# Eight sparse tiles of a graph layer, fetched row by row by SyncE instead of by GpSimd

## The chip, the cores and the metric

One core of a Trainium2 chip runs the kernel. The metric is the device time of one execution, in microseconds (us). Five engines work side by side, each through its own program in order: TensorE (PE in the profile; its weight loads PEld), VectorE (DVE), ScalarE (ACT), GpSimd (POOL) and SyncE (SP), which only issues transfers. They wait for each other by semaphores. A transfer adds 16 to its semaphore when it has landed.

## The reference

A graph with 12500 nodes of 128 features and 200000 edges, sorted by destination, each with a type of 9. The message of an edge is its source's row through a linear layer plus an embedding of its type; messages are summed by destination, and a GRU cell with the node's own row gives the update; the result is added to x and normalized.

```python
src_h = h[src] @ W_msg.T + b_msg
emb = edge_embed[jnp.clip(edge_type, 0, NUM_EDGE_TYPES)]
msg = src_h + emb
messages = jax.ops.segment_sum(msg, dst, num_segments=num_nodes)
h_new = _gru_cell(messages, h[:num_nodes], W_ih, W_hh, b_ih, b_hh)
...
x = _layernorm(x + _L0_gnn_ref(x, edge_index, edge_type_9, ...), axis=-1)
```

## The kernel before, in words

As the layers are linear, the kernel sums the sources' rows and the counts of edge types for each destination first, and applies the weights to the sums. The destinations are treated in two ways.

*Dense part.* The first 3328 nodes have about half of the edges. For them one-hot matrices are made on VectorE (items `B`, lines 862 to 887), turned into a matrix of counts on TensorE (line 1099), copied to SBUF by ScalarE (line 1226), and multiplied with all of x (items `F`, line 1114). This needs no fetching of rows.

*Sparse part.* The other edges stand in 764 tiles (`NG`) of 128 edges, four to a group, 191 groups (`GROUPS`). For each tile the 128 source rows are fetched to a buffer of `xg`, which has 17 (`RING`): GpSimd issues one indirect DMA a tile (`gather`, line 601, recorded at line 604), after a wait on `s_used` for the buffer 17 tiles back to be free. The first 22 groups (`SWITCH`) fetch the fp32 rows of x itself. The others fetch from `x_split`, a tensor in HBM in which each row of x stands as three bf16 parts, 768 bytes in all, and which SyncE writes at the start from SBUF (lines 542 to 550, semaphore `s_xw`). TensorE multiplies the three parts of each tile with a one-hot matrix (line 1081) and adds `G` = 4 to `s_used` behind each group's last product (line 1085). VectorE adds each group's sums to a ring (line 906), at an offset from a register: it loads four such offsets at a time (line 890).

*Final stages.* The nodes are finished in 49 blocks (`NBLK`) of 256, in the order `ORDER`. A block passes the stages `cn`, `hh`, `su`, `rz`, `t2`, `th`, `yt`, `bn`, `sd`, `ln`: two sets of products on TensorE (`hh`, line 1042, reads the block's transposed rows `xb` and the weights `whh`; `su`, lines 1056 and 1059), the gates on ScalarE and VectorE, `yt` on VectorE (lines 818 to 820, reads the block's own rows `xn` and raises `s_y`), and the norm, whose last step `ln` (line 837) writes a store buffer and raises `s_ln`.

*Order.* Dense items, sparse groups and final stages are woven into one list, `ITEMS`, by `schedule` (line 193), and TensorE, VectorE and ScalarE go through it in order. SyncE's program, once `x_split` is written, is `finish` (line 552): for each block, load `xb` (two buffers; from the third block on after `hh` two blocks back), wait for the `yt` of the block before, load `xn` (one buffer), and, from the third block on, wait for the `ln` two blocks back and store that block. A block of the dense part is stored in 16 pieces (line 504), another in one (line 506). TensorE waits for `xb` before `hh` (line 1040), VectorE for `xn` before `yt`, and for a store two blocks back before `ln`.

*Weights.* `wih` and `wms` hold input weights that are needed by the item `weights` (lines 1027 and 1028) only; it stands behind group 10, and VectorE's last step of it raises `s_wc`.

A second path (`slow`) is taken if a property of the data does not hold; it isn't taken here.

Of the kernel before, what the change touches and what calls it, by code (L numbers as in the profile page):

```python
# [5 lines left out]
N, H, E, NT = 12500, 128, 200000, 9  # L6
P = 128
G = 4
# [9 lines left out]
HT = NT + 1  # L18
HC = HT + HI
TAIL = N - (HI - 1) * P  # L20
SPREAD = math.sqrt(E * math.sqrt(ND / N) * (1 - math.sqrt(ND / N)))
T0 = int((E * math.sqrt(ND / N) - 3.5 * SPREAD) // (G * P)) * G
TC = int((E * math.sqrt(ND / N) + 4.5 * SPREAD) // P) + 2
NG = TILES - T0
GROUPS = NG // G
# [3 lines left out]
RING = 17  # L29
# [16 lines left out]
UNITS = -(-HI // XU)  # L46
# [4 lines left out]
SWITCH = 22  # L51
# [14 lines left out]
BF16 = mybir.dt.bfloat16  # L66
F16 = mybir.dt.float16
F32R = mybir.dt.float32r
I32 = mybir.dt.int32
# [4 lines left out]
ET = mybir.EngineType  # L74
# [201 lines left out]
ITEMS, LB, UB, LATE = schedule()  # L276
WG = [width(g) for g in range(GROUPS)]
ORDER = [it[2] for it in ITEMS if it[0] == "hh"]
POS = {b: i for i, b in enumerate(ORDER)}
STORES = [BN // RUN if b < CB0 else 2 if b == NBLK - 1 else 1 for b in ORDER]  # L280


# [30 lines left out]
    return max([j + 1 for j in range(i) if table_of(j, slow)], default=0)  # L313


def gnn_kernel(nc, x, xT, xN, srcT, dstT, typT, dstG, dstC, dstS, dstB, rec, srcA, typA, dstE, low, table, masks,
               wmsg, bmsg, embT, wihT, whhT, bih, bhh, out):
    ctx = ExitStack()
    with ctx:
        def sb(name, shape, dt=F32):  # L320
            return ctx.enter_context(nc.sbuf_tensor(name, shape, dt))
# [4 lines left out]
        def sem(name):  # L326
            return ctx.enter_context(nc.semaphore(name))
# [60 lines left out]
        spare = sb("spare", [P, 1])  # L388
        mm = sb("mm", [P, 2, 2])
        wms = sb("wms", [P, H])  # L390
        embs = sb("embs", [P, ND2])
        bmc = sb("bmc", [P, 1])
        mask = sb("mask", [P, 2])
        wih = sb("wih", [P, 3 * H])
        wihc = sb("wihc", [P, 3 * H])
        whh = sb("whh", [P, 3 * H])
        emw = sb("emw", [P, 4 * H], F32R)
# [20 lines left out]
        def late(n):  # L418
# [28 lines left out]
        names = ("s_idx s_gl s_dt s_tl s_lb s_w s_io s_id s_d s_mg s_sg s_bg s_fl s_tab s_dc s_so "  # L447
                 "s_blk s_ptr s_z s_bad s_sum s_prm s_tm s_te s_cp s_si s_st "
                 "s_bi s_em s_cn s_used s_oh s_acc s_ok s_kd s_eb s_fd s_toh s_tr s_sl s_main "
                 "s_e18 s_wp s_wc s_xn s_hh s_pm s_rz s_t2 s_n s_y s_mv s_sd s_ln s_xc s_p1 s_xe s_p2 s_xl s_xw s_nid s_sc s_tt s_xt s_tv").split()  # L450
        S = {n: sem(n) for n in names}
        s_g = [sem(f"s_g{i}") for i in range(RING)]
        s_o = [sem(f"s_o{i}") for i in range(2)]
        s_x = [sem(f"s_x{i}") for i in range(2)]
        s_xd = [sem(f"s_xd{i}") for i in range(4)]
# [3 lines left out]
        def xg32(slot):  # L459
            return xg[:, slot, 0:2 * H].bitcast(F32)  # L460
# [7 lines left out]
        def second(i, slow):  # L468
            return not slow and i in SECOND
# [26 lines left out]
        def store(sp, i):  # L496
            b = ORDER[i]
            n0 = b * BN
            yo = yos[i % 2]
            sp.wait_ge(S["s_ln"], i + 1)  # L500
            if b < CB0:
                for k in range(BN // RUN):
                    n, p = NODES[n0 + k * RUN], k * RUN % P
                    sp.dma_start(out[n:n + RUN, :], yo[p:p + RUN, k * RUN // P, :]).then_inc(s_o[i % 2], 16)
            elif b < NBLK - 1:
                sp.dma_start(out[n0:n0 + BN, :].rearrange("(s p) h -> p s h", s=2), yo[:, :, :]).then_inc(s_o[i % 2], 16)
            else:
                sp.dma_start(out[n0:n0 + P, :], yo[:, 0, :]).then_inc(s_o[i % 2], 16)
                sp.dma_start(out[n0 + P:N, :], yo[0:N - n0 - P, 1, :]).then_inc(s_o[i % 2], 16)
# [3 lines left out]
        @block.sync  # L513
        def _(sp):
            sp.dma_start(coarseI, dstC.partition_broadcast(P)).then_inc(S["s_dc"], 16)

            def load_x(u):
                if u >= 4:
                    sp.wait_ge(S["s_p1"], u - 3)
                h0, h1 = unit(u)  # L520
                full = min(h1, HI - 1)
                sp.dma_start(x1[:, u % 4, 0:(full - h0) * H].rearrange("p (h f) -> p h f", f=H),
                             x[h0 * P:full * P, :].rearrange("(h p) f -> p h f", p=P)).then_inc(s_xd[u % 4], 16)
                if full < h1:
                    sp.dma_start(x1[0:TAIL, u % 4, (full - h0) * H:(h1 - h0) * H],
                                 x[full * P:N, :]).then_inc(s_xd[u % 4], 16)

            load_x(0)
            load_x(1)
            sp.dma_start(gI[:, :, :], dstG).then_inc(S["s_gl"], 16)  # L530
            load_x(2)
            load_x(3)
            sp.dma_start(typI, typT).then_inc(S["s_tl"], 16)
            sp.dma_start(sortI, dstS).then_inc(S["s_so"], 16)
            sp.dma_start(dstI, dstT).then_inc(S["s_dt"], 16)
            sp.dma_start(lbF, low).then_inc(S["s_lb"], 16)
            for u in range(4, UNITS):
                load_x(u)
            sp.wait_ge(S["s_fl"], 1)
            bad = read_flag(ET.SP)  # L540

            def split_out(u):
                h0, h1 = unit(u)
                full = min(h1, HI - 1)
                sp.wait_ge(S["s_xl"], u + 1)
                sp.dma_start(x_d[h0 * P:full * P, :].rearrange("(h p) f -> p h f", p=P),
                             xs[:, h0:full, :, :].rearrange("p h c f -> p h (c f)")).then_inc(S["s_xw"], 16)
                if full < h1:
                    sp.dma_start(x_d[full * P:N, :],
                                 xs[0:TAIL, full, :, :].rearrange("p c f -> p (c f)")).then_inc(S["s_xw"], 16)  # L550

            def finish(slow):
                sp.wait_ge(S["s_xl"], UNITS)
                for i, b in enumerate(ORDER):
                    if i > 1:
                        sp.wait_ge(S["s_hh"], i - 1)
                    sp.dma_start(xb[:, i % 2, :], xT[:, b * BN:(b + 1) * BN]).then_inc(s_x[i % 2], 16)
                    if second(i, slow):
                        if gone(i, slow):
                            sp.wait_ge(S["s_y"], gone(i, slow))  # L560
                        else:
                            sp.wait_ge(S["s_fd"], NQ)
                        sp.dma_start(xn1[:, :, :], xN[b]).then_inc(S["s_xt"], 16)
                    else:
                        if i:
                            sp.wait_ge(S["s_y"], gone(i, slow))
                        sp.dma_start(xn[:, :, :], xN[b]).then_inc(S["s_xn"], 16)
                    if 1 < i < NBLK - 2:
                        store(sp, i - 2)
                for i in range(NBLK - 4, NBLK):  # L570
                    store(sp, i)
                for i in (NBLK - 2, NBLK - 1):
                    sp.wait_ge(s_o[i % 2], stored(i))

            with sp.If(bad == 0):
                for u in range(UNITS):
                    split_out(u)
                finish(False)
            with sp.Else():
                finish(True)  # L580

        @block.gpsimd
        def _(pool):
# [14 lines left out]
                pool.wait_ge(S["s_z"], 5 + k)  # L598
            pool.wait_ge(S["s_idx"], 16)

            def gather(p, split, idx=idx):
                if p >= RING:
                    pool.wait_ge(S["s_used"], p - RING + 1)
                pool.indirect_dma_start(  # L604
                    out=xg[:, p % RING, :] if split else xg32(p % RING), out_offset=None, in_=x_d if split else x,
                    in_offset=bass.IndirectOffsetOnAxis(ap=idx[:, p:p + 1], axis=0),
                ).then_inc(s_g[p % RING], 16)

            for p in range(FIRST):
                gather(p, False)  # L610
# [15 lines left out]
            bad = read_flag(ET.Pool)  # L626
            with pool.If(bad == 0):
                pool.wait_ge(S["s_xw"], 16 * (UNITS + 1))
                for p in range(SWITCH * G, NG):
                    gather(p, True)  # L630
            with pool.Else():
                pool.wait_ge(S["s_si"], 16)
                for p in range(SWITCH * G, TILES):
# [342 lines left out]
        def _(pe):  # L976
# [86 lines left out]
            with pe.If(bad == 0):  # L1063
                pe.wait_ge(S["s_id"], 2)
                for it in ITEMS:
                    if it[0] == "G":
# [5 lines left out]
                            pe.wait_ge(S["s_acc"], BEFORE[("GA", g - 1)] + 1)  # L1072
                        for j in range(G):
                            p = g * G + j
                            pe.wait_ge(s_g[p % RING], 16 * (p // RING + 1))
                            if g < SWITCH:
                                ins = pe.matmul(g2[:, 0, 0:w], xg32(p % RING), oh[:, j, :], start=(j == 0),  # L1077
                                                stop=(j == G - 1), skip_group_check=True)
                            else:
                                for c in range(3):  # L1080
                                    ins = pe.matmul(g2[:, 0, 0:w], xg[:, p % RING, c * H:(c + 1) * H], oh16[:, j, :],  # L1081
                                                    start=(j == 0 and c == 0), stop=(j == G - 1 and c == 2),
                                                    skip_group_check=True)
                        for j in range(G):
# [236 lines left out]
```

## Time and profile before

| | |
|---|---|
| Median of 3 runs | 1030.05 us (1030.01 to 1031.35) |
| Profiled execution, its own time | 1030.4 us |
| Its span, first to last instruction | 1028.5 us |
| Mean granted TensorE clock | 0.972 |
| TensorE busy | 941.9 us (92%), 8241 matmuls |
| VectorE busy | 844.2 us (82%) |
| ScalarE busy | 625.3 us (61%) |
| GpSimd busy | 762.4 us (74%), of it 728.7 us in 764 gathers |
| Transfers | 114 GB/s over the span |

A row of the page's fifth part names a group of instructions by line and engine, how often it ran, its busy time, and how long the engine had been idle just before such instructions and what ended that. A list of waits sums such idle times by who waited for whom. "Issue" there is time in which the profile shows nothing that was waited for. A timeline has one row for an instruction, or for several alike that follow each other. SPq, DVEq and the like are the engines' queues: transfers issued, register loads and register arithmetic, which do not count as busy time.

### The profile page before, as it was taken

How to read it: one execution, taken by the hardware profiler on the slowest of the kernel's cores; microseconds unless marked ns; L12 is line 12 of the kernel's file. 1: busy time of each engine (PE TensorE's matmuls, PEld its weight loads, DVE VectorE, ACT ScalarE, POOL GpSimd, SP SyncE). 2: the span in 40 equal slices, each digit the busy share in tenths (PEclk: the TensorE clock that was granted, in tenths of full speed). 3: DMA queues.
4: the chain of work that ended last, by engine and by line, in shares of the span. 5: the costliest groups of instructions: out<-in, count | busy, mean ns of one | idle time of the engine just before them, and what ended most of it. 6: DMA issues, size and time to landing. Idle time of an engine off the chain costs nothing.

```text
span 1028.5 us, 23000 instructions
## 1 busy us (share of the span) xinstructions
PE 941.9 (92%) x8241; PEld 621.8 (60%) x8241; DVE 844.2 (82%) x2678; ACT 625.3 (61%) x1207; POOL 762.4 (74%) x807
## 2 busy tenths in 40 slices
PE   5789899999999999999999999999999999999963
PEld 2256566666666656666666666666666666666641
DVE  8788888897989979987899788888888988886463
ACT  4664257665676567656676666767676667566231
POOL 7777777777777777777777777777777777777771
PEclk9888999999999999999999999999999999999986
DMA  8889223333334333334343433434343433343441
GB/s 268 232 248 303 55 63 89 94 97 93 106 85 111 94 97 103 103 93 110 80 108 99 111 94 96 109 96 110 97 109 93 112 94 105 101 112 99 106 128 43
DMA packets 95666, 116.98 MB, mean 114 GB/s; under 512 B 20027, under 2 KB 81271, under 8 KB 95544
## 3 DMA queue, kind: packets, MB, share of 16 engines
q0 software_dynamic: 36608, 75.94, 28.0%
q1 hardware_dynamic: 57080, 37.80, 12.5%
q10 hardware_dynamic: 1856, 1.68, 0.5%
q8 instruction: 68, 1.11, 0.5%
q14 instruction: 54, 0.44, 0.1%
HBM read 99.34 MB, written 16.00 MB: 112 GB/s over the span
## 4 chain that ended last, share of the span: by engine, by line
PE 66%; DVE 9%; ACT 7%; POOL 7%; issue 6%; DMA 4%; POOLq 0%; DVEq 0%; ACTq 0%; SPq 0%
PE psf L1114 30%; PE psb L1099 13%; POOL xg L604 7%; PE pAB L1042 5%; PE pAB L1056 5%; PE psg L1081 5%; ACT mem L1226 3%; DMA arena<-in_x 2%; PE psg L1077 2%; PE psg L1085 2%; PE pAB L1059 2%; DVE ohk L877 2%; DVE ohl L883 1%; ACT L1213 1%; DVE ohk L880 1%
## 5 line engine op out<-in xcount | busy, mean ns | idle before, releaser
L604 POOL DMA_INDIRECT xg<-x_split,idx x676 | 642.9, 951 | 206.0 <-issue 195.6
L1114 PE MATMUL psf<-mem 128*128 128x384 bf16 x2548 | 562.0, 327 | 7.4 <-ACT arena L1236 6.6
L1226 ACT CAST mem<-psb 128x432 f16<-128x432 f32 x832 | 400.3, 522 | 222.2 <-PE psb L1099 210.8
L1099 PE MATMUL psb<-ohk,ohl 128*128 128x108 bf16 (+3 forms) x1801 | 385.7, 258 | 17.4 <-ACT mem L1226 16.6
L877 DVE TENSOR_TENSOR ohk<-table_bank,prm 128x392 bf16<-128x392 f16 (+3 forms) x421 | 260.6, 619 | 64.1 <-PE psb L1099 61.8
L1114 PEld LDWEIGHTS psf<-mem 128*128 128x128 f16 x2548 | 219.3, 98 | 107.2 <-issue 18.9
L1099 PEld LDWEIGHTS psb<-ohk,ohl 128*128 128x128 bf16 x1801 | 165.9, 99 | 138.4 <-ACT mem L1226 31.1
L883 DVE TENSOR_TENSOR ohl<-table_bank,prm 128x512 bf16<-128x512 f16 x421 | 174.4, 414 | 0.0
L1081 PE MATMUL psg<-ohs,xg 128*128 128x56 bf16 (+9 forms) x2028 | 97.1, 196 | 12.7 <-DMA xg<-x_split,idx 8.5
L604 POOL DMA_INDIRECT xg<-in_x,idx x88 | 85.8, 975 | 29.6 <-issue 24.4
L1081 PEld LDWEIGHTS psg<-ohs,xg 128*128 128x128 bf16 x2028 | 86.4, 97 | 30.6 <-DMA xg<-x_split,idx 9.8
L880 DVE TENSOR_TENSOR ohk<-table_bank,sort 128x40 bf16<-128x40 f16 (+3 forms) x421 | 102.6, 244 | 0.0
L906 DVE TENSOR_TENSOR mem<-mem,psg 128x120 f32 (+10 forms) x191 | 55.9, 293 | 47.9 <-PE psg L1085 33.5
L856 DVE TENSOR_TENSOR ohs<-rel,table_bank 128x240 f32<-128x240 f16 (+10 forms) x191 | 83.4, 437 | 0.6 <-issue 0.5
L1042 PE MATMUL pAB<-whh,xb 128*128 128x384 f32 x188 | 72.4, 509 | 0.0
L1205 ACT ACTIVATE arena<-pAB 128x512 f32<-128x512 f32 x47 | 28.1, 597 | 64.8 <-PE pAB L1059 64.7
L1213 ACT ACT_TABLE_LOAD x47 | 60.3, 1283 | 0.9
L1205 ACT ACT_TABLE_LOAD x47 | 60.3, 1283 | 0.8
L1085 PE MATMUL psg<-ohs,tohb 128*128 128x60 bf16 (+10 forms) x764 | 56.6, 196 | 0.0
L1056 PE MATMUL pAB<-wihc,mem 128*128 128x384 f32 x136 | 50.2, 492 | 0.2 <-DVE cnts L796 0.2
L1208 ACT ACTIVATE arena<-arena 128x256 f32<-128x256 f32 x47 | 19.6, 418 | 42.7 <-DVE arena L811 42.4
L1042 PEld LDWEIGHTS pAB<-whh,xb 128*128 128x128 f32 x188 | 34.3, 197 | 15.4 <-issue 1.2
(148 smaller groups left out, 799.3 us busy)
## 6 DMA issues: line engine op xcount, KB each, us to landing
xg<-x_split,idx POOLq DMA_INDIRECT x676
x_split<-mem SPq DMA_DIRECT2D x24, 384.0 KB
xb<-in_xT SPq DMA_DIRECT2D x49, 128.0 KB
arena<-in_x SPq DMA_DIRECT2D x24, 256.0 KB, 7.2
arena<-in_xN SPq DMA_DIRECT2D x47, 128.0 KB
out<-arena SPq DMA_DIRECT2D x18, 128.0 KB
out<-spill SPq DMA_DIRECT2D x17, 128.0 KB
out<-spill SPq DMA_DIRECT2D x112, 8.0 KB
```

The lines of the kernel that those rows point to most:

```text
L604: pool.indirect_dma_start(out=xg[:, p % RING, :] if split else xg32(p % RING), out_offset=None, in_=x_d if split else x, in_offset=bass.In ...
L856: v.tensor_tensor(onehots(g)[0], rel[:, g, :].unsqueeze(2).to_broadcast([P, G, w]), count_up[:, 0:w].unsqueeze(1).to_broadcast([P, G, w]), ...
L877: v.tensor_tensor(nodes[:, :, :, HT:HC], numbers[:, :, HT:HC].unsqueeze(1).to_broadcast([P, k, m, HI]), key[:, a:a + k, :].unsqueeze(2).to ...
L880: v.tensor_tensor(nodes[:, :, :, 0:HT], numbers[:, :, HT:2 * HT].unsqueeze(1).to_broadcast([P, k, m, HT]), sort[:, a:a + k].unsqueeze(2).u ...
L883: v.tensor_tensor(ohl[:, a % KB:a % KB + k, :].rearrange("p k (c t) -> p k c t", t=2), count_up[:, 0:P].rearrange("p (c t) -> p c t", t=2) ...
L1042: ins = pe.matmul(pAB[:, s, H:4 * H], xb[:, i % 2, s * P:(s + 1) * P], whh[:, :], start=True, stop=False, skip_group_check=True)
L1056: pe.matmul(pAB[:, s, 0:3 * H], sums[:, s * P:(s + 1) * P], wihc[:, :], start=False, stop=False, skip_group_check=True)
L1081: ins = pe.matmul(g2[:, 0, 0:w], xg[:, p % RING, c * H:(c + 1) * H], oh16[:, j, :], start=(j == 0 and c == 0), stop=(j == G - 1 and c == 2 ...
L1099: ins = pe.matmul(psb[:, bank % NB, held * HC:(held + m) * HC], ohl[:, e % KB, :], ohk[:, e % KB, d * HC:(d + m) * HC], start=(k == 0), st ...
L1114: pe.matmul(psf[:, 0:3 * H], Bb[q % 2][0:kk, HT + h, :], xs[0:kk, h, :, :].rearrange("p c f -> p (c f)"), start=(h == 0), stop=(h == HI - ...
L1205: act.activation(rz[:, :, :], pAB[:, :, H:3 * H], ACT.Sigmoid).then_inc(S["s_rz"], 1)
L1226: act.copy(Bb[q % 2][:, :, n:n + MOST], psb[:, bank % NB, 0:MOST * HC].rearrange("p (d h) -> p h d", h=HC)).then_inc(S["s_eb"], 1)
```

## The change

Of the 764 tiles, eight (`BY_ROW`), each the last tile of a group, are left out of GpSimd's list (`BY_POOL`), and its other tiles take the 17 buffers in turn by their place in that list (`PLACE_OF`). The eight groups are `ROW_G` = 45, 68, 87, 107, 125, 143, 161 and 177. SyncE fetches these tiles: for each of the 128 rows one transfer of 768 bytes from `x_split` to one partition, with the row number in a register. The buffers are two, `rowx`, in the place of the weights `wih`, and the row numbers of a tile are loaded from a new input `srcR` to the first partition of `wms`, and from there to registers four at a time. In `finish`, from the third block on, 9 rows (`PER`) are issued at each of three places of a block: behind the load of `xb`, behind that of `xn`, and behind the store. Before the first row SyncE waits for `s_wc` and `s_xw`, and before the first row of a tile from the third tile on for the group of the tile two back; it also waits for the tile's row numbers to land. TensorE waits for a row tile by `s_row`, 16 for each row, and reads `rowx` instead of `xg`.

```diff
+BY_ROW = 8
+FINALS = 5
+PER = 9
...
+def row_groups():
+    out = []
+    for j in range(BY_ROW):
+        last = ORDER[2 + FINALS * (j + 1) - 1]
+        at = next(k for k, it in enumerate(ITEMS) if it[0] == "ln" and it[1] == POS[last])
+        out.append(1 + next(it[1] for it in ITEMS[at:] if it[0] == "G"))
+    return out
+
+
+ROW_G = row_groups()
+ROW_OF = {g * G + G - 1: j for j, g in enumerate(ROW_G)}
+BY_POOL = [p for p in range(NG) if p not in ROW_OF]
+PLACE_OF = {p: n for n, p in enumerate(BY_POOL)}
...
+        row_i = wms[0:1, :].bitcast(I32)
...
+        rowx = wih[:, :].bitcast(BF16).rearrange("p (k c) -> p k c", k=2)
...
+            def by_row(count):
+                for n in range(sent[0], min(sent[0] + count, BY_ROW * P)):
+                    j, r = divmod(n, P)
+                    if n == 0:
+                        sp.wait_ge(S["s_wc"], 1)
+                        sp.wait_ge(S["s_xw"], 16 * (UNITS + 1))
+                    if r == 0:
+                        if j >= 2:
+                            sp.wait_ge(S["s_used"], G * (ROW_G[j - 2] + 1))
+                        sp.dma_start(row_i, srcR[j:j + 1, :]).then_inc(S["s_ri"], 16)
+                        sp.wait_ge(S["s_ri"], 16 * (j + 1))
+                    if r % 4 == 0:
+                        _, vals = nc.values_load_multi_w_load_instructions(
+                            row_i[0:1, r:r + 4], engines=[ET.SP], min_val=0, max_val=N - 1,
+                            skip_runtime_bounds_check_because="a source is a node")
+                        nodes.update(enumerate(vals))
+                    sp.dma_start(rowx[r:r + 1, j % 2, :], x_d[bass.ds(nodes[r % 4], 1), :]).then_inc(s_row[j % 2], 16)
+                    sent[0] = n + 1
...
                     sp.dma_start(xb[:, i % 2, :], xT[:, b * BN:(b + 1) * BN]).then_inc(s_x[i % 2], 16)
+                    if not slow and i >= 2:
+                        by_row(PER)
...
                         sp.dma_start(xn[:, :, :], xN[b]).then_inc(S["s_xn"], 16)
+                    if not slow and i >= 2:
+                        by_row(PER)
                     if 1 < i < NBLK - 2:
                         store(sp, i - 2)
+                    if not slow and i >= 2:
+                        by_row(PER)
...
-                for p in range(SWITCH * G, NG):
-                    gather(p, True)
+                for n in range(SWITCH * G, len(BY_POOL)):
+                    gather(BY_POOL[n], True, n=n)
...
-                            pe.wait_ge(s_g[p % RING], 16 * (p // RING + 1))
+                            if p in ROW_OF:
+                                pe.wait_ge(s_row[ROW_OF[p] % 2], 16 * P * (ROW_OF[p] // 2 + 1))
+                                parts = rowx[:, ROW_OF[p] % 2, :]
+                            else:
+                                n = PLACE_OF[p]
+                                pe.wait_ge(s_g[n % RING], 16 * (n // RING + 1))
+                                parts = xg[:, n % RING, :]
...
-                                    ins = pe.matmul(g2[:, 0, 0:w], xg[:, p % RING, c * H:(c + 1) * H], oh16[:, j, :],
+                                    ins = pe.matmul(g2[:, 0, 0:w], parts[:, c * H:(c + 1) * H], oh16[:, j, :],
```

## Rows read from the trace of the kernel before

**Rows 1.** The page, parts 1 and 4: busy time by engine; shares of the chain.

```profile
PE 941.9 (92%) x8241; PEld 621.8 (60%) x8241; DVE 844.2 (82%) x2678; ACT 625.3 (61%) x1207; POOL 762.4 (74%) x807
...
PE 66%; DVE 9%; ACT 7%; POOL 7%; issue 6%; DMA 4%; POOLq 0%; DVEq 0%; ACTq 0%; SPq 0%
```

**Rows 2.** List of waits, GpSimd, whole span: engine, line, releaser; us, times, longest us.

```profile
POOL xg L604 <- issue: 220.0, 722, 0.3
POOL xg L604 <- PE psg L1085: 15.2, 41, 3.0
```

**Rows 3.** Timeline, GpSimd, 500 to 504 us: start, us, engine, line, operation, tiles [idle before].

```profile
500.17 0.95 POOL L604 DMA_INDIRECT xg<-x_split,idx  x1 [0.30 <-issue]
501.42 0.95 POOL L604 DMA_INDIRECT xg<-x_split,idx  x1 [0.30 <-issue]
```

**Rows 4.** Groups by line, TensorE, 927 to 1012 us; columns as in part 5 of the page.

```profile
L1081 PE MATMUL psg<-ohs,xg 128*128 128x88 bf16 x210 | 13.7, 210 | 12.0 <-DMA xg<-x_split,idx 8.5 <-issue 3.4
```

**Rows 5.** The chain in order of time, its end: start us, us, what.

```profile
1007.79 3.67 DMA xg<-x_split,idx
```

**Rows 6.** Timeline, TensorE, 1009 to 1013 us.

```profile
1011.51 0.30 PE L1081 MATMUL psg<-ohs,xg 128*128 128x88 bf16 x3 [1.39 <-DMA xg<-x_split,idx]
```

**Rows 7.** Windows, TensorE, two stretches: length, busy us, matmuls, granted clock, DMA share, GB/s.

```profile
170.60:644.60 474.00, 454.30 (x4325) 1.00 0.37 99
644.60:899.10 254.50, 245.18 (x2221) 1.00 0.39 103
```

**Rows 8.** List of waits, SyncE's own queue, whole span.

```profile
SPq L567 <- DVE arena L820: 734.1, 46, 39.6
```

**Rows 9.** Timeline, SyncE: `xn` loads (line 567) of chosen blocks, and two whole rounds.

```profile
170.58 0.33 SPq L567 DMA_DIRECT2D arena<-in_xN  x1
...
388.19 0.33 SPq L567 DMA_DIRECT2D arena<-in_xN  x1
388.56 0.44 SPq L506 DMA_DIRECT2D out<-arena  x1
389.04 0.47 SPq L557 DMA_DIRECT2D xb<-in_xT  x1
404.10 0.33 SPq L567 DMA_DIRECT2D arena<-in_xN  x1
404.47 8.27 SPq L504 DMA_DIRECT2D out<-spill  x16
412.79 0.42 SPq L557 DMA_DIRECT2D xb<-in_xT  x1
...
644.56 0.33 SPq L567 DMA_DIRECT2D arena<-in_xN  x1
...
645.41 0.47 SPq L557 DMA_DIRECT2D xb<-in_xT  x1
...
899.06 0.33 SPq L567 DMA_DIRECT2D arena<-in_xN  x1
```

**Rows 10.** By line: operation, count, ns least/median/most, first and last start us.

```profile
L504 SPq DMA_DIRECT2D out<-spill x112: 314/420/1387, 274.9 to 1005.0; - x112
...
L536 SPq DMA_DIRECT2D ohs<-in_low x1: 343/343/343, 7.8 to 7.8; - x1
...
L493 SPq TENSOR_LOAD <-flag x1: 521/521/521, 61.1 to 61.1; - x1
...
L890 DVEq TENSOR_LOAD <-gbI x48: 339/343/1202, 68.1 to 1000.6; - x48
...
L906 DVEq FUSED_REGOPS  x191: 57/57/65, 71.2 to 1012.0; - x191
L906 DVE TENSOR_TENSOR mem<-mem,psg x191: 236/290/340, 71.3 to 1012.1; 128x112 f32 x19, 128x120 f32 x19, 128x136 f32 x19, 128x152 f32 x19
```

**Rows 11.** Timeline, TensorE, 667 to 669 us: the product that reads `xb` of block 27.

```profile
667.41 1.52 PE L1042 MATMUL pAB<-whh,xb 128*128 128x384 f32 x4
```

**Rows 12.** The page, part 6: KB of each issue, median us to landing.

```profile
mem<-in_xN SPq DMA_DIRECT2D x2, 128.0 KB, 3.0
```

More of the change, by code:

```diff
@@ L279 @@
 POS = {b: i for i, b in enumerate(ORDER)}
+def row_groups():
[9 more added lines that the diff above has]
+PLACE_OF = {p: n for n, p in enumerate(BY_POOL)}
+assert min(ROW_G) >= SWITCH and max(ROW_G) < GROUPS - 3 and 3 * FINALS * PER >= P
 STORES = [BN // RUN if b < CB0 else 2 if b == NBLK - 1 else 1 for b in ORDER]
@@ L313, in last_count, with gnn_kernel @@
     return max([j + 1 for j in range(i) if table_of(j, slow)], default=0)
-def gnn_kernel(nc, x, xT, xN, srcT, dstT, typT, dstG, dstC, dstS, dstB, rec, srcA, typA, dstE, low, table, masks,
+def gnn_kernel(nc, x, xT, xN, srcR, srcT, dstT, typT, dstG, dstC, dstS, dstB, rec, srcA, typA, dstE, low, table, masks,
                wmsg, bmsg, embT, wihT, whhT, bih, bhh, out):
@@ L449, in gnn_kernel @@
                  "s_bi s_em s_cn s_used s_oh s_acc s_ok s_kd s_eb s_fd s_toh s_tr s_sl s_main "
-                 "s_e18 s_wp s_wc s_xn s_hh s_pm s_rz s_t2 s_n s_y s_mv s_sd s_ln s_xc s_p1 s_xe s_p2 s_xl s_xw s_nid s_sc s_tt s_xt s_tv").split()
+                 "s_e18 s_wp s_wc s_xn s_hh s_pm s_rz s_t2 s_n s_y s_mv s_sd s_ln s_xc s_p1 s_xe s_p2 s_xl s_xw s_nid s_sc s_tt s_xt s_tv s_ri").split()
         S = {n: sem(n) for n in names}
         s_g = [sem(f"s_g{i}") for i in range(RING)]
+        s_row = [sem(f"s_row{i}") for i in range(2)]
         s_o = [sem(f"s_o{i}") for i in range(2)]
@@ L550, in split_out @@
                                  xs[0:TAIL, full, :, :].rearrange("p c f -> p (c f)")).then_inc(S["s_xw"], 16)
+            sent, nodes = [0], {}
+            def by_row(count):
[16 more added lines that the diff above has]
+                    sent[0] = n + 1
             def finish(slow):
@@ L599, in _, with gather @@
             pool.wait_ge(S["s_idx"], 16)
-            def gather(p, split, idx=idx):
-                if p >= RING:
-                    pool.wait_ge(S["s_used"], p - RING + 1)
+            def gather(p, split, idx=idx, n=None):
+                n = p if n is None else n
+                if n >= RING:
+                    pool.wait_ge(S["s_used"], (BY_POOL[n - RING] if split else n - RING) + 1)
                 pool.indirect_dma_start(
-                    out=xg[:, p % RING, :] if split else xg32(p % RING), out_offset=None, in_=x_d if split else x,
+                    out=xg[:, n % RING, :] if split else xg32(n % RING), out_offset=None, in_=x_d if split else x,
                     in_offset=bass.IndirectOffsetOnAxis(ap=idx[:, p:p + 1], axis=0),
-                ).then_inc(s_g[p % RING], 16)
+                ).then_inc(s_g[n % RING], 16)
             for p in range(FIRST):
@@ L1290 @@
         "xN": lay(placed.reshape(NBLK, 2, P, H).transpose(0, 2, 1, 3).reshape(NBLK, P, 2, H)),
+        "srcR": lay(np.stack([turned(src, 0)[p * P:(p + 1) * P] for p in sorted(ROW_OF)])),
         "srcT": rows(src, 0, sparse),
```

## The prediction

> **What bounds the kernel now.** I read the page first: its busy shares and its chain. TensorE is busy 92% of the span, GpSimd 74%, and the chain that ended last is two thirds TensorE, with 7% on GpSimd's gathers [rows 1]. GpSimd's 74% misleads. In the list of waits GpSimd's idle time before its 764 gathers is 220.0 us of "issue" in 722 pieces of at most 0.3 us, and only 15.2 us behind TensorE [rows 2]. The timeline shows what that is: one gather every 1.25 us, 0.95 us of work and 0.30 us between two [rows 3]. 764 x 1.25 = 955 us, so from its first tens of microseconds to its last gather at 1007.79 [rows 5] GpSimd has no pause. It is a second bound, as long as the kernel, and TensorE runs just behind it. Over most of the span neither holds the other up; at the end, when the dense work has run out, TensorE does wait: 12.0 us before the products of the gathered tiles between 927 and 1012 us [rows 4]. The last gather lands 3.67 us after its start [rows 5], its product starts at 1011.51 [rows 6], and some 17 us of final stages follow up to 1028.5. TensorE has no room elsewhere: it is busy 454.3 of 474.0 us and 245.2 of 254.5 us in the two stretches that matter below [rows 7].
>
> **What the change removes.** Eight gathers leave GpSimd: 8 x 1.25 = 10.0 us [rows 3]. Each of TensorE's 12.0 us of waiting at the end [rows 4] is for a gather that would then be there up to 10.0 us earlier. So the gain is bounded by 10.0 us above and by nothing below (if something else holds TensorE up); I take 9 us, since the eight leave one by one and the last waits are spread over 80 us. TensorE's matmuls for the eight tiles are the same, from another buffer. The bytes fetched are the same, too.
>
> **What it adds: 1024 issues on SyncE.** SyncE looks free: it waits 734.1 us, in 46 pieces, for VectorE to be done with a block's `y` before it reloads `xn` [rows 8]. It now gets, from the third block on, three times 9 rows a block: 27 a block, used up after 38 blocks. What is one row worth?
> - The issue. The nearest row is a load to a single partition, 0.343 us; the 16-partition stores have a median of 0.420 [rows 10]. Between two neighbours lie 0.04 us (388.19 + 0.33 to 388.56 [rows 9]). That is 0.38 us.
> - Hiccups. Sixteen stores took 8.32 us, 0.52 each, where 0.46 would be median and gap [rows 9, 10]: now and then one issue takes 0.9 us more. I take 0.04 us a row.
> - The address. The trace before has no SyncE transfer with an address from a register. VectorE's addition with such an address has a register instruction of 57 ns in front and starts 0.1 us after it [rows 10]. Bounds: 0 (hidden beside the issue before) to 0.2 us (two such). I take 0.10, the one row there is.
> - The row numbers, four at a time. VectorE's loads of four take 0.343 us in the median, SyncE's one load of one value 0.521 [rows 10]; with a gap of 0.04, a quarter is 0.10 to 0.14 us. I take 0.10, as 48 loads say more than one.
>
> Sum: c = 0.38 + 0.04 + 0.10 + 0.10 = 0.62 us a row. Ends: 0.314 (the least issue [rows 10]) + 0.04 + 0.10 = 0.45, and 0.42 + 0.04 + 0.06 + 0.2 + 0.14 = 0.86. The Trainium skill ("DMA: Bandwidth & Descriptors", Latency and other measured facts) gives a register load a floor of about 600 ns. The trace contradicts it for VectorE (0.343 us); by the page's figure, as an estimate, a row would cost 0.06 us more and the kernel some 60 us more than I forecast.
>
> 1024 x 0.62 = 635 us is less than 734 us, so at first sight it fits. But SyncE's idle time cannot be saved up: its program waits for each block's `y`, and what matters is the room from one `xn` load to the next. In the timeline these loads stand at 170.58 (third block), 644.56 (the 26th) and 899.06 (the 41st) [rows 9]: 474.0 / 23 = 20.6 us a block, then 254.5 / 15 = 17.0 us. Against that a block asks for
> - its own issues, 388.19 to 389.51 = 1.3 us [rows 9];
> - where the store is of 16 pieces, 8.27 instead of 0.44 us, 7.8 more [rows 9]: 7 of the first 23 blocks and 4 of the 15, so 2.4 and 2.1 us;
> - one load of 128 row numbers per tile, with its landing waited for on the queue: 0.4 + 3.0 us [rows 12] over 4.7 blocks, 0.7 us;
> - 27 x 0.62 = 16.7 us.
>
> That is 21.1 of 20.6 us in the first stretch, a backlog of 0.5 x 23 = 12 us, and 20.8 of 17.0 in the second, 3.8 x 15 = 57 us. Who is queued behind the rows? `xb`, `xn` and the stores. `xn` has a whole block of slack. `xb` is next: in the program it now stands behind 18 rows of the iteration before. For block 27 it was issued at 645.41 [rows 9] and its product started at 667.41 [rows 11], 22.0 us; take off 18 x 0.62 = 11.2 and a landing of 3.0 [rows 12], and 7.8 us of backlog are free. Beyond it TensorE, whose program is in order, stands at `hh` (line 1042). 12 + 57 - 8 = 61 us. Walking the 38 blocks one by one with the trace's times of `y`, `ln` and `hh` (long blocks idle, short ones overflow) gives 59 us with a landing of 2.5 us, 66 with 3.0; I take 62.
>
> The stalls on `xb` come before the end and give GpSimd time to fill its 17 buffers, so the 12.0 us of waiting for gathers vanish in any case: 62 - 12 = 50. The row tiles themselves come in time in that walk (the first 14 us, the later ones over 20 us before their group). The waits for `s_wc` and `s_xw` are over when the first row is due at about 137 us, and those for `s_used`, two tiles back, too. On the profiled execution, 1030.4 us around a span of 1028.5, that is 1080; its time is 0.3 us over the median of the runs shown, which is nothing here.
>
> **Rivals.**
> - *Faster: SyncE keeps pace.* The same walk stalls for 0 to 1 us at c = 0.48 and 6 to 10 us at 0.52; the point where stalls eat the gain of 12 is c = 0.53. It needs the register arithmetic to be hidden and the small load to be the cheap one: 0.38 + 0.10 = 0.48. For it: 0.314 and 0.343 us are the trace's own rows [rows 10]. Against it: the 57 ns [rows 10] are spent in order on VectorE. Time 1030.4 - 9 = 1021.
> - *Between:* c of 0.53 to 0.57, 9 to 34 us of stalls less 12, so 1027 to 1053.
> - *Slower by far:* two register instructions a row, or the dear load. c = 0.70 stalls 131 to 139 us, so about 1153.
> - *Nothing moves,* because GpSimd's work is not the bound and SyncE has room: 1030. The row that speaks against it is the 12.0 us [rows 4]. The Trainium skill has a rule that would give this result ("DMA: Bandwidth & Descriptors", Issuing engines are not separate DMA queues): issuing from several engines saves only the sequencer's time, "which is usually small relative to the DMA itself". Here one gather takes its engine 1.25 us at a stretch of 955, so by the trace the sequencers' time is the matter on both engines.
>
> **How the numbers follow.** Chances: c of 0.58 to 0.67 (the forecast, its own range 1053 to 1130) 0.52; faster 0.25; between 0.08, of which half within 0.2%; far slower 0.15, "nothing moves" being counted in the half of "between". The forecast is the likeliest case, 1080. The range reaches down over the fast case, whose end is 1019 (10.0 us and a little of noise), and up to 1130, where c is 0.67: 0.15 above and 0.02 below are left out. By over 0.2% (2 us, what a measurement of this kernel can tell): faster 0.25, same 0.04, slower 0.71.
>
> **What will show it.** In the timeline of SyncE, the pitch of the row transfers: 0.62 us each on average with register work; below 0.53 the fast case holds. The list of SyncE's waits should shrink from 734 us to under 150. TensorE should wait at line 1042 for `xb`, first around blocks 20 to 26, most in blocks 28 to 39, and no longer for `xg` at the end. GpSimd should wait for TensorE's release of `xg`. If TensorE waits for `rowx` at its groups instead, or VectorE for `xn` at line 818, the place is wrong though the cause is right; if the row pitch is as said and nobody waits, the walk is wrong.

## The result and the profile after

The changed kernel takes 1052.5 us in the median of four runs (1047.6 to 1054.9), beside 1030.7 us for the kernel before on the same chips. The ratio is 1.019, with a 95% interval of 1.017 to 1.021: slower by 22 us. The direction was forecast, the size was not: 1080 was said. The profiled execution took 1054.2 us, 23.8 more than that of before.

The page of the changed kernel, parts 1 and 4:

```profile
PE 952.2 (90%) x8241; PEld 626.6 (60%) x8241; DVE 845.0 (80%) x2678; ACT 625.4 (59%) x1207; POOL 754.6 (72%) x799
...
PE 44%; SPq 28%; issue 11%; DVE 9%; ACT 4%; DMA 2%; POOL 1%; DVEq 0%; ACTq 0%
```

No computing engine has more instructions than before; TensorE's 8241 matmuls took 10.3 us more [rows 1], at a mean granted clock of 0.960 instead of 0.972. The chain that ended last [rows 1] now runs for 28% of the span through SyncE's queue, which had no part in it; by line it is the row transfers (line 592, 15%), the loads of row numbers (line 588, 7%) and the stores (line 526, 4%).

Lists of waits of the changed kernel: TensorE's first, then GpSimd's, SyncE's own queue and one of VectorE's.

```profile
PE pAB L1092 <- DMA xb<-in_xT: 18.6, 4, 8.8
```

```profile
POOL xg L654 <- PE psg L1141: 55.9, 66, 10.1
```

```profile
SPq L612 <- DVE arena L870: 169.8, 16, 42.9
```

```profile
DVE rs L885 <- DMA out<-arena: 7.5, 2, 3.8
```

TensorE waits 18.6 us for `xb` at `hh` (line 1092, which was 1042 and had no such wait). GpSimd, which waited 15.2 us for TensorE [rows 2], now waits 55.9, up to 10.1 at a time: it is no longer a bound. SyncE's waits for `y` fell from 734.1 [rows 8] to 169.8 us, and from 46 pieces to 16: for most blocks it comes to the `xn` load late. VectorE waits 7.5 us at the last step of two blocks for stores that free its buffer: the waits end at 763.2 and 838.6 us, each some 2 us after the last piece of a 16-piece store that SyncE had begun behind rows.

The timeline of SyncE around one of the waits (start, us, operation) and the product that waited:

```profile
754.91 6.44 SPq L526 DMA_DIRECT2D out<-arena  x14
761.53 4.78 SPq L592 DMA_DIRECT2D wih<-x_split  x9
766.37 0.37 SPq L600 DMA_DIRECT2D xb<-in_xT  x1
766.93 4.75 SPq L592 DMA_DIRECT2D wih<-x_split  x9
771.73 0.37 SPq L612 DMA_DIRECT2D arena<-in_xN  x1
```

```profile
768.57 2.90 PE L1092 MATMUL pAB<-whh,xb 128*128 128x384 f32 x4 [5.50 <-DMA xb<-in_xT]
```

Sixteen pieces of a store (14 of them lie in the window shown), nine rows, and only then `xb`, at 766.37. TensorE's product starts 2.2 us later, after 5.5 us of standing. Its four products then take 2.90 us, where the like four took 1.52 before [rows 11]: from 767.6 to 774.2 us the granted clock is 0.50, the lower level of 1.2 GHz. Between `xb` and `xn` lie nine rows in 5.0 us, 0.55 us each.

What a row costs, by line (count: ns least/median/most):

```profile
L588 SPq TENSOR_LOAD <-wms x256: 458/554/724, 142.7 to 931.5; - x128
...
L592 SPq FUSED_REGOPS  x1024: 37/37/51, 143.2 to 933.5; - x171
L592 SPq MOVE wih<-x_split x1024: 29/29/29, 143.3 to 933.5; - x171
L592 SPq DMA_DIRECT2D wih<-x_split x1024: 224/228/299, 143.3 to 933.6; - x171
```

The mean distance of neighbouring row transfers, over the 903 pairs with no other transfer between them, is 0.575 us.

### The profile page after: what moved, and what is told of

Its sections match the earlier page's. It is cut to its first block, busy times and chain, and to the rows that moved or that the text cites. A ratio compares the mean times of both kernels' runs of the same rounds, so it can differ in the third digit from the quotient of the medians.

```text
span 1052.4 us, 26331 instructions
## 1 busy us (share of the span) xinstructions
PE 952.2 (90%) x8241; PEld 626.6 (60%) x8241; DVE 845.0 (80%) x2678; ACT 625.4 (59%) x1207; POOL 754.6 (72%) x799
## 4 chain that ended last, share of the span: by engine, by line
PE 44%; SPq 28%; issue 11%; DVE 9%; ACT 4%; DMA 2%; POOL 1%; DVEq 0%; ACTq 0%
PE psf L1170 19%; SPq L592 15%; PE psb L1155 8%; SPq L588 7%; SPq L526 4%; PE pAB L1092 4%; PE pAB L1106 3%; PE psg L1137 3%; PE psg L1133 2%; ACT mem L1282 2%; DVE ohk L715 1%; DVE ohk L927 1%; PE psg L1141 1%; PE pAB L1109 1%; DVE ohl L933 1%
## 5 line engine op out<-in xcount | busy, mean ns | idle before, releaser
L654 POOL DMA_INDIRECT xg<-x_split,idx x668 | 635.4, 951 | 236.4 <-issue 185.0
L1170 PE MATMUL psf<-mem 128*128 128x384 bf16 x2548 | 567.7, 329 | 7.4 <-ACT arena L1292 6.6
L956 DVE TENSOR_TENSOR mem<-mem,psg 128x120 f32 (+10 forms) x191 | 55.9, 293 | 49.7 <-PE psg L1141 44.6
L1092 PE MATMUL pAB<-whh,xb 128*128 128x384 f32 x188 | 74.4, 521 | 18.6 <-DMA xb<-in_xT 18.6
```

Of the source, the lines that this page charges most:

```text
L654: pool.indirect_dma_start(out=xg[:, n % RING, :] if split else xg32(n % RING), out_offset=None, in_=x_d if split else x, in_offset=bass.In ...
L1092: ins = pe.matmul(pAB[:, s, H:4 * H], xb[:, i % 2, s * P:(s + 1) * P], whh[:, :], start=True, stop=False, skip_group_check=True)
L1170: pe.matmul(psf[:, 0:3 * H], Bb[q % 2][0:kk, HT + h, :], xs[0:kk, h, :, :].rearrange("p c f -> p (c f)"), start=(h == 0), stop=(h == HI - ...
```

## The experiments

Theory: the loss is SyncE's time. If 27 rows and the other issues of a block take longer than the block, SyncE falls behind, `xb` comes late, and TensorE stands at `hh`. What it costs is estimated from the price c of a row by the walk over the blocks of the prediction, a small model whose steps are not printed here; its figures below are estimates. Rivals: the 1024 small transfers disturb others or fill a queue; the waits at the row tiles; the loss goes with the number of transfers, not with SyncE's time.

**e1_drop: what eight gathers are worth.**

```diff
                     if r == 0:
...
-                        sp.dma_start(row_i, srcR[j:j + 1, :]).then_inc(S["s_ri"], 16)
-                        sp.wait_ge(S["s_ri"], 16 * (j + 1))
-                    if r % 4 == 0:
-                        _, vals = ...
-                    sp.dma_start(rowx[r:r + 1, j % 2, :], x_d[bass.ds(nodes[r % 4], 1), :]).then_inc(s_row[j % 2], 16)
+                        sp.dma_start(rowx[:, j % 2, :], x_d[j * P:(j + 1) * P, :]).then_inc(s_row[j % 2], 16)
...
-                                pe.wait_ge(s_row[ROW_OF[p] % 2], 16 * P * (ROW_OF[p] // 2 + 1))
+                                pe.wait_ge(s_row[ROW_OF[p] % 2], 16 * (ROW_OF[p] // 2 + 1))
```

> The changed kernel, but SyncE fetches each of the eight tiles by one plain transfer of 128 neighbouring rows, so the tiles hold other rows than the reference's and almost nothing is added to SyncE. It shows what taking eight gathers off GpSimd is worth by itself. The prediction's step (each of the 12.0 us of waiting at the end is given back, up to 10.0): about 1021, 9 us under before. Rival, from the trace of the changed kernel, where 7.2 us of such waiting are left although TensorE was held up for 18.6 us earlier: the last groups are consumed faster than one gather in 1.25 us and only 17 buffers can be filled ahead, so only 4 to 5 us come back, 1025 to 1026. Second rival: nothing, 1030.

Measured: 1025.2 us (ten runs, 1020.7 to 1029.1) beside 1030.5, ratio 0.995 (0.993 to 0.997): 5.3 us, not 9. TensorE's waits at the sparse products after 930 us, in its list of waits:

```profile
PE psg L1130 <- issue: 7.2, 3, 3.8
```

Of the 12.0 us of before [rows 4], 7.2 are left, and none is put down to a gather any more. GpSimd now waits for TensorE for 27.4 us in all. So eight gathers are worth 5 us, and something else holds TensorE for the rest; the first rival's number was right, its reason (17 buffers) is dealt with below.

**e2_cost: the rows without the relief.** GpSimd gathers all 764 tiles and TensorE reads those; SyncE issues its 1024 rows, and waits for them only at its end.

```diff
-BY_POOL = [p for p in range(NG) if p not in ROW_OF]
+BY_POOL = list(range(NG))
...
+                if not slow:
+                    for k in range(2):
+                        sp.wait_ge(s_row[k], 16 * P * (BY_ROW // 2))
...
-                            if p in ROW_OF:
-                                pe.wait_ge(s_row[ROW_OF[p] % 2], ...)
-                                parts = rowx[:, ROW_OF[p] % 2, :]
-                            else:
...
```

> SyncE issues the 1024 row transfers as in the changed kernel, but GpSimd gathers all 764 tiles and TensorE reads those; nobody waits for the rows before the end. It shows the cost of the issues alone. Theory (SyncE's queue delays xb): TensorE waits 18 to 25 us at the hh products, first around block 28, and the total is that of the changed kernel within 5 us, 1047 to 1058, since a TensorE that is late there no longer waits as long for gathers. Rival (the gathers of GpSimd are what is lost, or the waits for the row tiles): 1030 to 1035.

Measured: 1055.2 us (1049.6 to 1058.8), ratio 1.024 (1.019 to 1.029). The list of waits of TensorE begins with

```profile
PE pAB L1095 <- DMA xb<-in_xT: 19.0, 4, 8.8
```

four waits as in the changed kernel, at the same four blocks. The loss is in SyncE's issues, whatever becomes of the rows: neither the waits at the row tiles nor GpSimd's new list have a part in it.

**e3_const: the same transfers, cheaper to issue.**

```diff
-                        sp.dma_start(row_i, srcR[j:j + 1, :]).then_inc(S["s_ri"], 16)
-                        sp.wait_ge(S["s_ri"], 16 * (j + 1))
-                    if r % 4 == 0:
-                        _, vals = ...
-                    sp.dma_start(rowx[r:r + 1, j % 2, :], x_d[bass.ds(nodes[r % 4], 1), :])...
+                    sp.dma_start(rowx[r:r + 1, j % 2, :], x_d[n:n + 1, :])...
```

> The changed kernel with row numbers fixed in the program (rows 0 to 1023 in turn, so the tiles hold other rows than the reference's): the same 1024 single-row transfers, but no register load and no register arithmetic. Theory: a row costs SyncE some 0.27 us instead of 0.57, the walk over the blocks has no stall, no wait at hh, and the time equals that of e1_drop within 1 us. Rival (1024 small transfers on one DMA ring disturb the others, or fill the queue): the stalls stay, 1040 to 1055.

Measured: 1027.0 us (ten runs, 1021.1 to 1027.8), ratio 0.995 (0.993 to 0.997), like e1_drop. A row takes 0.303 us on average, and TensorE does not wait for `xb` at `hh`. 1024 small transfers alone do not bring the loss. The rows here lie side by side in memory, unlike the reference's; e4_load16 shows the same with the reference's rows, and with it this rival is out.

**e4_load16: the change with a cheaper row.**

```diff
-                    if r % 4 == 0:
+                    if r % 16 == 0:
...
-                            row_i[0:1, r:r + 4], ...
+                            row_i[0:1, r:r + 16], ...
```

> The changed kernel, with 16 row numbers loaded at a time instead of four. Theory: if the load of 0.554 us is mostly a fixed round trip, a row costs 0.41 + 0.04 to 0.08 = 0.45 to 0.50 us, the walk's stalls are 0 to 3 us, and the time is 1022 to 1030, so faster than before by up to 0.5%. If the load's time goes with its registers (2.2 us for 16), a row costs as before and the time stays at 1048 to 1055.

Measured: 1024.3 us (ten runs, 1020.5 to 1029.6), ratio 0.994 (0.992 to 0.997); in a second set of runs, on another chip, 1026.4 (e11_load16_again), ratio 0.996 (0.994 to 0.998). The load by line:

```profile
L588 SPq TENSOR_LOAD <-wms x64: 1132/1224/1446, 141.8 to 895.1; - x64
```

Sixteen numbers in 1.224 us, against four in 0.554: the row falls from 0.575 to 0.491 us on average, and with it goes the whole loss of 27 us against e1_drop. It fetches the same rows as the changed kernel, and it is faster than both kernels. This is the sharpest sign of a threshold: 0.084 us less a row, 86 us less of SyncE's time, are worth 26 to 28 us, and the way from 0.491 to 0.303 (e3_const) is worth nothing.

**e5_xb_act: another queue for `xb`.** ScalarE issues the load, behind the gates of the block two before.

```diff
-                    if i > 1:
-                        sp.wait_ge(S["s_hh"], i - 1)
-                    sp.dma_start(xb[:, i % 2, :], xT[:, b * BN:(b + 1) * BN]).then_inc(s_x[i % 2], 16)
+                    if slow or i < 2:
+                        ...
...
+                    if not slow and i + 2 < NBLK:
+                        b = ORDER[i + 2]
+                        act.wait_ge(S["s_hh"], i + 1)
+                        act.dma_start(xb[:, i % 2, :], xT[:, b * BN:(b + 1) * BN]).then_inc(s_x[i % 2], 16)
```

> The changed kernel, but ScalarE issues the loads of xb from the third block on, right behind the gates of the block two before, so xb is no longer queued behind SyncE's rows. Theory: the next transfer behind the rows is xn; TensorE no longer waits at the hh products, VectorE waits before yt instead, in the blocks around 31 to 39. The walk over the blocks gives 18 to 19 us of stalls where it gives 30 for the changed kernel, so 1025 (e1_drop) + 17 = about 1042. Rival (xb's queueing is all of the loss): 1025 to 1028. Rival (the queueing is not the cause): 1052 as before the edit.

Measured: 1038.9 us (1036.7 to 1040.2), ratio 1.009 (1.006 to 1.011). The group of `hh` products, and what VectorE waits for before `yt` and before its last step:

```profile
L1093 PE MATMUL pAB<-whh,xb 128*128 128x384 f32 x188 | 72.3, 509 | 0.0
```

```profile
DVE rs L886 <- DMA out<-arena: 7.4, 2, 5.0
DVE arena L869 <- DMA arena<-in_xN: 6.7, 2, 3.7
```

TensorE waits for `xb` no more, and 14 us are back. What is left goes with the waits for `xn`, 6.7 us, which no one had waited for in the changed kernel, and for stores, 7.4 us, as there. The edit also takes the issue of `xb` off SyncE, some 0.4 us a block, so not all of the 14 us need be the place in the queue. `xb`'s place behind the rows is where the loss entered, and SyncE's shortage of time is the cause.

**e6_five: fewer rows a block.**

```diff
-BY_ROW = 8
-FINALS = 5
-PER = 9
+BY_ROW = 5
+FINALS = 8
+PER = 6
```

> The changed kernel with five row tiles instead of eight and 6 rows at a place, so 18 rows a block instead of 27, at the same price of a row. Theory: 18 x 0.575 = 10.4 us of rows and 4.1 of other work fit into the 17.0 us of a block in the tight stretch; no stall at hh. Five gathers are 6.2 us of GpSimd's time; if only some 5 us of waits for gathers can come back, five tiles give nearly all of it, 1025 to 1027. Rival (the loss is a cost per block or per tile, not the sum against the room): 1040 to 1050.

Measured: 1025.1 us (ten runs, 1022.2 to 1030.3), ratio 0.996 (0.994 to 0.998), at 0.547 us a row and with no wait at `hh`. Five tiles at the dear price bring what eight bring at the cheap one.

**e7_load2: a dearer row.** The load is of two numbers (`r % 2`).

> The changed kernel with two row numbers loaded at a time instead of four. From 0.554 us for four and 1.224 for sixteen a load of two should take about 0.44 us, so a row costs 0.43 + 0.24 = 0.67 us instead of 0.575. Theory: the room is exceeded from block 14 on; the walk gives 96 us of stalls, so 1025 + 87 to 96 = 1112 to 1121. Rival (the loss goes with the number of transfers or with the waits at the row tiles, not with SyncE's time): below 1070.

Measured: 1259.6 us (1258.2 to 1260.6), ratio 1.224, 140 us over what I expected. The load and TensorE's waits for `xb`:

```profile
L588 SPq TENSOR_LOAD <-wms x512: 634/731/990, 139.8 to 1141.2; - x171
```

```profile
PE pAB L1092 <- DMA xb<-in_xT: 151.5, 28, 15.1
```

Two numbers take 0.731 us, longer than four. My 0.44 was a line through the loads of four and of sixteen, and it does not hold here. A row cost 0.817 us on average, not 0.67. At 0.817 the walk gives 240 us of stalls, 1025 + 240 = 1265, and 1259.6 was measured. The size of the load was misjudged; the total agrees with the walk, but TensorE's waits for `xb` are 151.5 us and not 240. What the rest is stands below, under "What the walk leaves out".

**e8_drop12: four more gathers off GpSimd.** As e1_drop, with `BY_ROW = 12`, `FINALS = 3`, `PER = 15`.

> As e1_drop with twelve tiles instead of eight taken off GpSimd, each fetched by one plain transfer of other rows than the reference's. It asks what holds TensorE at the end once eight gathers are gone. Theory: VectorE, whose addition of the group before is late in its own program behind a block's gates; then four more gathers give nothing, 1025 within 1.5 us, and the 7.2 us of waiting at the sparse products stay. Rival (still the gathers, at 1.25 us each): up to 5 us faster again, 1020, and less waiting.

Measured: 1026.3 us (seven runs, 1022.1 to 1032.3), ratio 0.998 (0.995 to 1.001). The waits at the sparse products after 930 us are the same to a tenth:

```profile
PE psg L1130 <- issue: 7.2, 3, 3.8
```

Fifteen microseconds less on GpSimd instead of ten do not change them, and the time is no lower than e1_drop's. Once eight gathers are gone, the gathers are not the bound; nor is the number of buffers, for then the waits would have shrunk.

**e9_order and e10_before_order: what the 7.2 us are.** In e4_load16, the two longer waits and VectorE's work ahead of the first:

```profile
986.73 0.64 PE L1137 MATMUL psg<-ohs,xg 128*128 128x88 bf16 x12 [2.87 <-issue]
```

```profile
985.96 0.42 DVE L870 SCALAR_TENSOR_TENSOR arena<-arena 128x256 f32<-128x256 f32 x1
986.30 0.33 DVE L956 TENSOR_TENSOR mem<-mem,psg 128x176 f32 x1
```

```profile
1003.61 0.34 DVE L956 TENSOR_TENSOR mem<-mem,psg 128x176 f32 x1
```

```profile
1004.05 0.65 PE L1137 MATMUL psg<-ohs,xg 128*128 128x88 bf16 x12 [3.77 <-issue]
```

A group's products may start once VectorE has added the group before (line 956): TensorE's program waits on `s_acc` for it. Both times the products start 0.1 us after the end of that addition (986.63 and 1003.95), so that is what ended both waits. A wait of 2.86 us of this kind stood in the kernel before too: it ended at 981.02 us, and VectorE's addition at 980.92. Ahead of the first wait the addition stands in VectorE's program behind the `yt` of a block (line 870). The edit moves two groups ahead of it:

```diff
 ITEMS, LB, UB, LATE = schedule()
+for g, y in ((183, ("yt", 44, 45)), (187, ("yt", 46, 46))):
+    pair = [("G", g), ("GA", g)]
+    ITEMS = [it for it in ITEMS if it not in pair]
+    k = ITEMS.index(y)
+    ITEMS[k:k] = pair
```

> e4_load16 with groups 183 and 187 moved ahead in the list of items, from behind the yt of blocks 44 and 46 (in order of processing) to just before it, so that VectorE adds them before the yt, norm and last step of those blocks. It asks whether the 7.2 us that TensorE still waits at its sparse products once the gathers are early are waits for VectorE's addition of the group before. Theory: yes; of the two waits of 2.9 and 3.8 us some 1.8 and 3.1 us go (that is what VectorE does in between), and the time falls 3 to 5 us under that of e11_load16_again. Rival (the waits are for gathers, or for something else): they stay, the same time.

> The same move of the two groups in the kernel before. Theory: there the last gathers come at 1.25 us each and hold TensorE, so the move gives at most 1 us, 1029 to 1031; removing only one of two waits that end close together gives nearly nothing. Rival (VectorE's order alone was the bound at the end, and the gathers did not matter): 3 to 5 us faster than before.

> e4_load16 once more, on the chip and in the rounds of e9_order, to compare with it: 1022 to 1027.

Measured: e9_order 1023.9 us (1022.5 to 1024.4), e11_load16_again 1026.4 (1021.3 to 1028.5): 2.5 us apart in the medians, with ranges that overlap, so no difference that I would claim. e10_before_order 1029.4, ratio 1.000 (0.999 to 1.001): nothing, as expected; but as the same move brought nothing clear in e9_order either, this run does not tell what held the kernel before. In e9_order the waits are

```profile
982.09 0.64 PE L1142 MATMUL psg<-ohs,xg 128*128 128x88 bf16 x12 [1.04 <-issue]
985.38 0.64 PE L1142 MATMUL psg<-ohs,xg 128*128 128x88 bf16 x12 [1.13 <-issue]
...
1001.45 1.04 PE L1142 MATMUL psg<-ohs,xg 128*128 128x88 bf16 x12 [3.94 <-issue]
```

and VectorE's addition before the last of them is

```profile
1001.01 0.34 DVE L961 TENSOR_TENSOR mem<-mem,psg 128x176 f32 x1 [1.01 <-issue]
```

The first wait of 2.9 us became two of 1.0 and 1.1, so it was one for VectorE's order. The second went to the next group, behind the same work of VectorE, and the sum fell from 7.2 to 6.7 us only. That these are waits for VectorE is shown by the times of its additions and by the first move; the 3 to 5 us that I expected from it were not there.

## Why the prediction was right or wrong

**Right: the cause, the place, the direction.** "1024 x 0.62 = 635 us is less than 734 us, so at first sight it fits", but the room is to be counted block by block, as the prediction did: e4_load16 and e6_five stand on one side of the threshold, the changed kernel and e7_load2 on the other. The stalls are at `hh`, for `xb`, and the four waits that the profile shows are at the blocks in positions 29, 31, 35 and 39 counted from 0, as "most in blocks 28 to 39" has it; the earlier stalls, "first around blocks 20 to 26", did not come, at the lower price. GpSimd waits for TensorE and the row tiles come in time, as said. Missed in the list of who is late: the stores, on which VectorE waited 7.5 us. SyncE's waits for `y` fell to 169.8 us, not under 150.

**Wrong: the price of a row,** the term c = 0.62 us that carries the size. 0.575 us were measured. By its parts, each with its gap to the next instruction:

| part | said | measured |
|---|---|---|
| issue of the transfer | 0.38 | 0.27 (0.228 + 0.045) |
| address from a register | 0.10 | 0.14 (an arithmetic instruction of 0.037 and a move of 0.029, with gaps) |
| a quarter of a load of four | 0.10 | 0.145 (0.554 + 0.03) |
| hiccups | 0.04 | 0.02 |

Three of four were off by 0.04 us or more, and in part they cancel. The issue was read off the row of a single-partition load of 2292 bytes at 0.343 us, the nearest there was [rows 10]; single rows are cheaper than any SyncE transfer in the trace before, below even its least of 0.314. The load was taken from VectorE's 48 rows and not from SyncE's one; SyncE's own 0.521 us would have been nearer to 0.554. The Trainium skill ("DMA: Bandwidth & Descriptors", Latency and other measured facts) puts the floor of a register load at some 600 ns. On SyncE the median for four values, 0.554 us, comes near it and the least, 0.458 us, is under it, while VectorE stays at 0.34 us. I had called the Trainium skill contradicted on VectorE's rows alone. Beside c, the wait for the row numbers of a tile was too dear as well: 3.0 us were said, and SyncE waited 10.8 us for eight, 1.35 each.

**What 0.045 us are worth.** Beyond the threshold each 0.01 us a row costs up to 10 us (1024 rows), near it some 5. The walk gives 59 to 66 us of stalls at 0.62, and with all measured prices 30. The prediction's own walk had 34 at 0.57, so the price of a row alone makes at most 28 of these 32 us, by the walk. With measured prices the walk stands like this, each time over e1_drop, which has the relief and no rows. The medians are from sets of runs on different chips, where the kernel before took 1029.2 to 1030.7 us, so 1 or 2 us in the last column say nothing:

| kernel | us a row | walk | measured |
|---|---|---|---|
| e3_const | 0.303 | 0 | 1.7 |
| e4_load16 | 0.491 | 0 | -1.0 |
| e6_five (18 rows a block) | 0.547 | 0 | -0.2 |
| e5_xb_act (`xb` elsewhere) | 0.573 | 18 to 19 | 13.6 |
| changed kernel | 0.575 | 30 | 27.2 |
| e7_load2 | 0.817 | 240 | 234.3 |

**What the walk leaves out.** The totals agree better than their parts. TensorE from the `hh` of block 24 to that of block 40 (counted from 0), in the changed kernel and in e1_drop (stretch, length, busy us, matmuls, granted clock, DMA share, GB/s):

```profile
640.60:943.20 302.60, 274.33 (x2425) 0.97 0.36 96
```

```profile
638.50:917.80 279.30, 269.74 (x2425) 0.99 0.38 102
```

The stretch is 23.3 us longer for the same 2425 matmuls: 18.7 us more of idle time, which are the 18.6 us of waits for `xb`, and 4.6 us more of busy time, at the lower mean clock. The same for e7_load2 and e1_drop, from block 6 to block 40:

```profile
265.80:1147.10 881.30, 683.91 (x5791) 0.89 0.28 75
```

```profile
267.10:917.80 650.70, 626.42 (x5792) 0.99 0.38 101
```

230.6 us longer: 173.1 of idle time, of it 151.5 for `xb`, and 57.5 of busy time. So the walk sizes the standing too large (30 against 18.7 us, 240 against 173.1), and a slower TensorE, of which the prediction has no term, makes up for part of it. That its totals come near the measured ones is in part luck. Where exactly the walk is too long was not tried.

**Wrong: "the 12.0 us of waiting for gathers vanish in any case".** 4.8 of them vanished, and eight gathers are worth 5.3 us, not 9 or 12. The row itself said it [rows 4]: of the 12.0 us only 8.5 were put down to a transfer and 3.4 to "issue", and I counted all of them as gathers. And I did not say what is late next when the gathers are early. It is VectorE's addition of the group before, which partly hid behind the waits for gathers, and e8_drop12 shows that more relief of GpSimd brings nothing. The same holds for the rival "faster", whose 1021 should have been 1025.

**The sum with both mended:** 1030.4 + 30 - 5 = 1055, against 1054.2 of the profiled execution; by the paragraph above, the 30 is near as a total only. The measured median lies at the edge of the case that I had called "between" (c of 0.53 to 0.57, 1027 to 1053) and given 0.08; c of 0.575 was well within the ends of 0.45 and 0.86 that the prediction gave, and the border of the forecast's own band at 0.58 was drawn too sharply for a sum whose terms had not been seen on SyncE in this form.

**The rule against the change.** The Trainium skill ("DMA: Bandwidth & Descriptors", Issuing engines are not separate DMA queues) says that spreading transfers over engines saves only sequencer time, which is usually small. Here nothing but sequencer time is moved, and it decides in both directions: 5 us gained in e1_drop, 27 lost again at 0.575 us a row, none at 0.491.

## What to carry to other kernels

An engine that is idle for 70% of the time has room for work only where its program can put it: count the room between two of its waits in the tightest stretch, and price the new work with it. Beyond that room added time is paid for almost in full (from 0.575 to 0.817 us a row SyncE had 248 us more to issue, and the kernel took 207 us more), and below it is free (from 0.303 to 0.491); so when the price is uncertain by 20%, cut the dose first (five tiles instead of eight gave the whole gain here). Of a wait that is to vanish, read what ended it, piece by piece, and name the second-latest input before counting it as gain. And when a model gives the right total, look in the trace for its parts before trusting it.

## What the runs showed of the hardware that was not expected

- A load of two values to SyncE's registers takes longer (0.731 us) than one of four (0.554); sixteen take 1.224. Why two are dearer was not tried.
- A single-row transfer of 768 bytes is issued in 0.228 us with its address from a register, against 0.42 for a store of 16 rows [rows 10]; the address takes two instructions, not one.
- 1024 transfers of one row each, at one in 0.3 us (e3_const), left the time as it was: 1027.0 us beside 1025.2 of e1_drop, with ranges that overlap.
- Around the end of each of TensorE's three longer waits for `xb` (5.5, 8.8 and 3.6 us, ended at 768.6, 844.1 and 920.4) its granted clock was at the lower level, 1.2 GHz: 0.50 in 767.6 to 774.2, 839.2 to 849.2 and 921.2 to 924.4 us. In e1_drop, without such waits, two stretches of 3.4 us at that level lie between 740 and 890 us.
